# Attention with P times V in five rounds a head, issued in two places, and one partial sum moved to VectorE

## The reference

```python
# layer 0 (per batch, 16 heads of 32)
energy = jnp.einsum('bhqd,bhkd->bhqk', q, k)
att = jax.nn.softmax(energy, axis=-1) / D ** 0.5
out = jnp.einsum('bhqk,bhkd->bhqd', att, v)
...
# layer 1
attn = jax.nn.softmax(jnp.einsum('bhqd,bhkd->bhqk', q, k) * hd ** (-0.5), axis=-1)
o = jnp.einsum('bhqk,bhkd->bhqd', attn, v).transpose(0, 2, 1, 3).reshape(B, T, D)
x = x + bitlinear(o, w_proj, b_proj)
```

## Time and profile before

| | |
|---|---|
| median of three executions | 3016.07 us |
| the profiled execution | 3021.92 us |
| its span | 3020.1 us |
| TensorE busy | 2781.6 us, 92% |
| VectorE busy | 2246.9 us, 74% |
| GpSimd busy | 1987.6 us, 66% |
| ScalarE busy | 1839.4 us, 61% |

### The profile page before, as it was taken

The page is one execution under the profiler, slowest core; times in us unless marked ns, Lnnn a source line. Parts: engine busy times, 40 slices in busy tenths (PEclk is TensorE's granted clock), DMA queues, the critical chain, the costliest instruction groups (busy, mean ns, idle before and its releaser), DMA issues. The chain is left out here.

```text
span 3020.1 us, 70269 instructions
## 1 busy us (share of the span) xinstructions
PE 2781.6 (92%) x22313; PEld 1481.0 (49%) x22313; DVE 2246.9 (74%) x4482; ACT 1839.4 (61%) x3287; POOL 1987.6 (66%) x1677
## 2 busy tenths in 40 slices
PE   7899999999999989999569998998999899958998
PEld 6654466444755547454235444544444445524444
DVE  4777688776877778777667768776877787738997
ACT  3366655665556654666346676667666766657887
POOL 0288824886268841889438885887788688854441
PEclk9999999999999999999889999999999999979999
DMA  6122343223422324222133213322232222143000
GB/s 210 43 54 53 125 133 100 54 69 120 154 70 58 116 105 131 63 53 74 40 108 81 55 23 107 80 58 53 79 75 58 64 73 61 39 152 134 31 28 35
DMA packets 101853, 243.28 MB, mean 81 GB/s; under 512 B 18620, under 2 KB 24900, under 8 KB 100552
## 3 DMA queue, kind: packets, MB, share of 16 engines
q1 hardware_dynamic: 99784, 233.49, 27.1%
q0 software_dynamic: 1792, 6.33, 0.6%
HBM read 99.15 MB, written 38.88 MB: 46 GB/s over the span
## 5 line engine op out<-in xcount | busy, mean ns | idle before, releaser
L459 DVE TENSOR_REDUCE b_mxs<-ps 128x1 f32<-128x512 f32 x1024 | 636.2, 684 | 198.4 <-PE ps L340 197.3
L459 DVE TENSOR_REDUCE a_mxs<-ps 128x1 f32<-128x512 f32 x1024 | 635.4, 683 | 176.7 <-PE ps L340 175.5
L425 ACT ACTIVATE a_p<-ps 128x512 f32<-128x512 f32 x1024 | 530.4, 602 | 242.3 <-PE ps L354 237.1
L425 ACT ACTIVATE b_p<-ps 128x512 f32<-128x512 f32 x1024 | 533.5, 602 | 201.3 <-PE ps L354 196.2
L312 POOL TENSOR_TENSOR b_sum<-b_p 128x512 f32<-128x512 f32 x384 | 496.7, 1297 | 87.2 <-ACT b_p L425 86.8
L312 POOL TENSOR_TENSOR a_sum<-a_p 128x512 f32<-128x512 f32 x384 | 498.2, 1301 | 68.6 <-ACT a_p L425 68.3
L340 PE MATMUL ps<-b_k,b_q 96*128 96x512 f32 x1024 | 443.6, 438 | 33.7 <-DVE b_mxs L459 23.3
L340 PE MATMUL ps<-a_k,a_q 96*128 96x512 f32 x1024 | 417.9, 417 | 6.8 <-DVE a_mxs L459 3.7
L354 PE MATMUL ps<-b_q,b_k 98*128 98x512 f32 x1024 | 400.1, 425 | 11.0 <-ACT b_p L425 7.8
L354 PE MATMUL ps<-a_q,a_k 98*128 98x512 f32 x1024 | 396.2, 421 | 9.8 <-ACT a_p L425 9.8
L368 PE MATMUL ps<-a_p,a_vx 128*32 128x512 f32 x2048 | 372.1, 599 | 10.7 <-POOL a_sum L317 8.9
(11 more groups left out here) (267 smaller groups left out, 4157.3 us busy)
## 6 DMA issues: line engine op xcount, KB each, us to landing
a_q<-a_qh SPq DMA_DIRECT2D x128, 128.0 KB, 2.3
a_k<-a_kh SPq DMA_DIRECT2D x128, 128.0 KB, 2.3
b_q<-b_qh SPq DMA_DIRECT2D x128, 128.0 KB, 2.3
b_k<-b_kh SPq DMA_DIRECT2D x128, 128.0 KB, 2.4
a_p<-in_w_fc SPq DMA_DIRECT2D x12, 1024.0 KB, 8.5
a_kl<-in_x SPq DMA_DIRECT2D x4, 2048.0 KB, 8.4
a_q<-a_ql SPq DMA_DIRECT2D x64, 128.0 KB, 2.3
a_k<-a_kl SPq DMA_DIRECT2D x64, 128.0 KB, 2.3
```

The costliest lines, as they stand in the source:

```text
L425: act.activation(self.key_tile(u, kt), self.st[RING[CHUNKS * (k % NJ) + n]], ACT.Exp, scale=self.scale).then_inc(self.s_exp, 1)
L459: dve.reduce_max(self.mxs[:, c:c + 1], self.mx[RING[CHUNKS * j + c]], axis=AX.X).then_inc(self.s_mxr, 1)
```

## The change

It changes how the eight key tiles of a half are dealt to rounds and who adds what.

- A table `VALUES` says for each of five rounds what each column group does: a pair (half, key tile), or (half, SUM). Rounds 0 and 1 do six key tiles of half 0 with two sums, round 2 does the last two of half 0 and the first two of half 1, rounds 3 and 4 do the other six of half 1 with its two sums. All twenty places are filled: 16 key tiles and four sums.
- A sum now covers four key tiles. Three of the four sums are POOL's (`SUM_OF` 0, 1 and 3), of three additions each. The fourth, of key tiles 0 to 3 of half 1, is one VectorE instruction (`sum_four`), a `tensor_reduce` that reads four tiles which lie 512 elements (2048 bytes) apart, one element of each in turn, and writes 512 sums.
- On TensorE the rounds stand in two places: rounds 3 and 4 of the head before after step 2, rounds 0, 1 and 2 after step 6. The folds go ahead of them. The transposition of the maxima moves from step 3 to step 4.
- `fold` has two forms, since the sum stands in the last column group for half 0 and in the first for half 1.
- In layer 0, VectorE waits ahead of the first attention for a DMA (`s_gout[3]`).

```diff
+    VALUES = (((0, 0), (0, 1), (0, 2), (0, SUM)), ((0, 3), (0, 4), (0, 5), (0, SUM)), ((0, 6), (0, 7), (1, 0), (1, 1)),
+              ((1, SUM), (1, 2), (1, 3), (1, 4)), ((1, SUM), (1, 5), (1, 6), (1, 7)))
+    ROUNDS = len(VALUES)
+    SUM_OF = (0, 1, None, 2, 3)
+    LAST = (2, 4)
+    FREED = ((0, 0, 0, 1, 1, 1, 2, 2), (3, 3, 3, 3, 4, 4, 4, 4))
+    def sums(self, pool, N, r, i):
+
+        u, kt = self.VALUES[r][0][0], TT // 2 * (r in (1, 4))
+        tile = self.sum[:, self.SUM_OF[r], :]
+        pool.wait_ge(self.s_pv, self.ROUNDS * (N - 1) + r + 1 + self.PV_CREDIT)
+        for n in range(1, TT // 2):
+            pool.wait_ge(self.s_exp, CHUNKS * N + TT * u + kt + n + 1 + self.EXP_CREDIT)
+            if n > 1:
+                pool.wait_ge(self.s_part, 2 * (3 * N + i) + n - 1)
+            add = pool.tensor_tensor(tile, self.key_tile(u, kt) if n == 1 else tile, self.key_tile(u, kt + n), ALU.add)
+            add.then_inc(self.s_part if n < TT // 2 - 1 else self.s_sum, 1)
...
             if ok(k):
-                self.sums(pool, k, N, 0)
+                self.sums(pool, N, 0, 0)
+                self.sums(pool, N, 1, 1)
             if ok(k + 1):
                 self.value(pool, 4 * i + k + 1, N + 1, (k + 1) % 2)
             if ok(k):
-                self.sums(pool, k, N, 1)
+                self.sums(pool, N, 4, 2)
...
-                after_values = s in (0, 2, 5)
+                after_values = s in (3, 7)
...
-                if s == 1 and ok(k - 1):
+                if s == 2 and ok(k - 1):
                     self.out_transpose(pe, 2 * N - 2, 0)
-                    self.values_round(pe, k - 1, N - 1, 1, 1)
-                    self.values_round(pe, k - 1, N - 1, 1, 2)
-                if s == 3 and ok(k + 1):
+                    self.values_round(pe, k - 1, N - 1, 3)
+                    self.values_round(pe, k - 1, N - 1, 4)
+                if s == 4 and ok(k + 1):
                     pe.wait_ge(self.s_o, 2 * N + 1)
                     self.m_transpose(pe, N + 1, 0)
-                if s == 4 and ok(k - 1):
+                if s == 6 and ok(k - 1):
                     self.out_transpose(pe, 2 * N - 1, 1)
-                if s == 4 and ok(k):
+                if s == 6 and ok(k):
                     if ok(k + 1):
                         pe.wait_ge(self.s_mrow, N + 2)
-                    self.values_round(pe, k, N, 0, 0)
-                    self.values_round(pe, k, N, 0, 1)
-                if s == 7 and ok(k):
-                    self.values_round(pe, k, N, 0, 2)
-                    self.values_round(pe, k, N, 1, 0)
+                    for r in range(3):
+                        self.values_round(pe, k, N, r)
...
+    def sum_four(self, dve, N):
+        dve.wait_ge(self.s_exp, CHUNKS * N + TT + TT // 2 + self.EXP_CREDIT)
+        dve.wait_ge(self.s_pv, self.ROUNDS * (N - 1) + 3 + 1 + self.PV_CREDIT)
+        keys = self.p[:, :, :].rearrange("p a (h n) -> p (a h) n", h=2)[:, TT:TT + TT // 2, :]
+        dve.tensor_reduce(self.sum[:, self.SUM_OF[3], :], keys.rearrange("p t n -> p n t"), AX.X, ALU.add).then_inc(self.s_sum_dve, 1)
```

More of the change, by code:

```diff
@@ L209, in setup_pool @@
         fill(self.ones[:, :], 1.0)
[L211 to L216, removed]
+        fill(self.fold[:, :, :], 0.0)
+        for u, sums in enumerate((3 * HD, 0)):
+            for r in range(0, P, HD):
+                if r != sums:
+                    ch.mark(pool.affine_select(out=self.fold[:, u, 0:HD], in_=self.fold[:, u, 0:HD], compare_op=ALU.not_equal,
+                                               fill=1.0, base=-r, pattern=[[-1, HD]], channel_multiplier=1))
+                    ch.wait()
+            fill(self.fold[sums:sums + 1, u, HD:HD + 1], 1.0)
         assert ch.n == self.SET
@@ L239, in call @@
             ok = (lambda kk: 0 <= 4 * i + kk < H) if known else (lambda kk: True)
-            head(i, k, H * b + n, ok, 5 if known and n == H else STEPS)
+            head(i, k, H * b + n, ok, 7 if known and n == H else STEPS)
         if flat:
@@ L355, in scores, with values_round @@
                   self.q[j][0:98, u * HALF:(u + 1) * HALF], start=True, stop=True).then_inc(self.s_st, 1)
[L357 removed]
+    def values_round(self, pe, k, N, r):
         if r == 0:
[L360 to L371 removed]
+            pe.wait_ge(self.s_o, 2 * N + 1)
+            pe.wait_ge(self.s_vx, N + 1)
+        if r == self.LAST[0]:
+            pe.wait_ge(self.s_o, 2 * N + 2)
+        if r == 3:
+            pe.wait_ge(self.s_sum_dve, N + 1)
+        elif self.SUM_OF[r] is not None:
+            pe.wait_ge(self.s_sum, 3 * N + (0, 1, None, None, 2)[r] + 1)
+        for c, (u, kt) in enumerate(self.VALUES[r]):
+            rounds = [n for n in range(self.ROUNDS) if self.VALUES[n][c][0] == u]
+            tile, weights = ((self.sum[:, self.SUM_OF[r], :], self.ones[:, :]) if kt == self.SUM else
+                             (self.key_tile(u, kt), self.vx[k % 2][:, kt, :]))
+            mm = pe.matmul(self.ot[u][HD * c:HD * (c + 1), :], weights, tile, start=r == rounds[0], stop=r == rounds[-1])
+        mm.then_inc(self.s_pv, 1)
     def out_transpose(self, pe, U, u):
@@ L444, in head @@
                     upper()
[L445 to L446 removed]
+                if s == 3 and ok(k - 1):
+                    self.out_copy(act, N - 1, 1)
+                if s == 7 and ok(k):
+                    self.out_copy(act, N, 0)
                 if ok(k):
@@ L492, in head @@
                 a = 1 if s < 2 else 2
-                if ok(k + a):
-                    for c in range(2):
+                for c in range(2):
+                    if ok(k + a):
                         self.reduce_chunk(dve, N + a, (k + a) % NJ, (2 * s + c + CHUNKS - 4) % CHUNKS)
+                    if s == 6 and c == 0 and ok(k - 1):
+                        self.divide(dve, 2 * N - 1, 1, 4 * i + k - 1)
                 if s == 1 and ok(k + 1):
                     self.m_parts(dve, N + 1)
-                if s in (1, 4) and ok(k - 1):
-                    self.divide(dve, 2 * N - 2 + s // 4, s // 4, 4 * i + k - 1)
+                if s == 2 and ok(k - 1):
+                    self.divide(dve, 2 * N - 2, 0, 4 * i + k - 1)
+                if s == 6 and ok(k):
+                    self.sum_four(dve, N)
                 if spare and ok(k) and not ok(k + 2) and (s >= 2 or not ok(k + 1)):
```

59 lines of the change are left out of this document (16 added, 43 removed).

## The result

| | before | after |
|---|---|---|
| median of four executions | 3018.53 us (3015.41 to 3026.71) | 3206.72 us (3203.92 to 3212.26) |
| span of the profiled execution | 3020.1 us | 3202.1 us |
| mean granted TensorE clock | 0.973 | 0.931 |

The ratio is 1.0621 with a 95% interval of 1.0593 to 1.0649: 188 us slower. The forecast was 2956 us, and its range ended at 3120.

A forecast was written before the change was run, and what follows sets the result against it. TensorE was taken to bound, 14.5 of 14.77 us a head. After the change, a POOL-TensorE-ScalarE chain (13.9), VectorE (13.6) and TensorE (13.35) gave 14.15 a head, 61 us saved, 2956 us; range 2938 to 3120, likeliest 2938 to 2971.

The forecast's parts named there:

- the price of `sum_four`: VectorE's reduction over four tiles, priced from a row over side-by-side elements (2286 ns) at 2.2 us net of overlap.
- the 3.1 us at which the sign turns: Reduction time from about which VectorE needs 14.4 us, a head takes 14.7, and the change makes the kernel slower.
- the likeliest range: The forecast's own case for the kernel's time, 2938 to 2971 us, chance 0.38.
- Rival A: VectorE's strided reduction is slow, 3.75 us; a head takes 15.4 us, the kernel 3095 us; chance 0.37.
- The loop: Chain through POOL (10.55 us), then TensorE and ScalarE (3.36 us), closing at the scores of step 7: 13.9 us a head.
- Rival B: POOL's additions stay 1.44 us apart, making the chain through three engines 14.3 us; 2972 to 2984 us; chance 0.16.
- the 0.1 to 0.5 named: Sign expected on TensorE: the second of the three rounds waits for POOL 0.1 to 0.5 us a head.
- VectorE's terms: VectorE's work a head: max reductions 9.6, maximum parts 0.54, divides 1.3, together 11.4 us; with the reduction at 2.2, 13.6.
- Three requirements lie close together: Per head, the chain through three engines needs 13.9 us, VectorE 13.6, TensorE 13.35; a head was taken as 14.15.
- small waits: The 0.3 us by which a head before the change exceeded TensorE's summed work, 14.5 us of 14.77.
- Rival C: POOL and VectorE hinder each other in SBUF, adding 0.7 us to the chain; 3010 to 3022 us; chance 0.05 with other cancellations.
- The last head: End of a batch, where TensorE makes no max chunks: the last head gives back 1.1 us of the gain per batch.

The follow-up runs named there:

- run 1: The changed kernel with VectorE's reduction summing four neighbouring elements instead of one from each of four tiles; sums not the softmax's; 2967.15 us, ratio 0.9824.
- run 3: The changed kernel with two reductions of two tiles each, 4096 bytes apart, in place of the one over four tiles; 2973.53 us in one execution.
- runs 2: The changed kernel with the reduction reading two neighbours of each of the four tiles, 2048 elements in, 256 sums out; 2964.11 us in one execution.
- run 10: The changed kernel with the four tiles interleaved in pairs (step of 8 bytes), the reduction reading two neighbours at each place; computes the reference; 2980.58 us, ratio 0.9864.
- Run 9: The changed kernel with three of a head's max chunks, just ahead of TensorE's wait for VectorE, issued twice; 3127.05 us, ratio 1.0341.
- run 13: The kernel of run 10 with one addition fewer in POOL's first sum of a head; results not the reference's; 2942.88 us, ratio 0.9744.
- run 11: The changed kernel with the reduction taking 508 sums of elements 2032 bytes apart instead of 2048; 3179.89 us in one execution.
- run 7: The changed kernel with VectorE's reduction made only in the first head of a batch; most outputs not the reference's; 2976.65 us, ratio 0.9848.
- run 14: The kernel of run 10 with round 2 behind step 7 instead of step 6; computes the reference; 2943.11 us, ratio 0.9741.
- run 4: The changed kernel with three VectorE additions in place of the reduction; results are the reference's; 3008.33 us, ratio 0.9961.

## Why the prediction was wrong

**The step that failed** is the price of `sum_four`: "The nearest row is the same instruction over 2048 elements that lie side by side, 2286 ns; I take it, 2.2 us net of overlap, since type, memory and count agree." Those three agree, but the order in which the elements are read does not, and it decides: 3.83 us for 2.28 (run 1). That is beyond the 3.1 us at which the sign turns. Run 1 has the order of the read alone put right, and the kernel comes in at 2967 us, inside the likeliest range. The contiguous row was called the nearest although it differs in the one thing that the change does anew.

The Trainium skill's page Vector Engine (DVE) Microarchitecture Reference, section 5.2 Measured stream behaviour on trn2, stood on the right side with its 1.73 ns a column for a source that hops every element; measured here 1.87 an element, whole instruction included. Its remark that a stream alternating between two regions keeps the full rate agrees with run 3 within a tenth (1.22 ns an element for 1.11 over neighbours), and its rule on adjacent pairs with runs 2 and 10. The error was to carry the remark from two places to four. The Trainium skill's page SBUF — State Buffer, section Specifications (TRN2), says of cachelines that each access that crosses to a new 16-byte line pays; run 3, in which every access does, shows almost no such cost, so it isn't that rule in this plain form.

**Rival A** was right in its mechanism and in its size: a reduction of 3.75 us (3.83), a head of 15.4 (15.33 at the full clock). That 3.75 lies so near is luck: it is four times a row of another instruction, with two inputs. What the rival lacked, and what took the time out of a range that held it, is the clock: the second step that failed is that every term was priced at a clock of 1.00. It gave 3095 us, and the kernel took 3207; 60 us of the middle heads are Rival A, 93 go with TensorE at 1.2 GHz. Run 9 gives 80 us back by adding work. The remaining 31 us, in first and last intervals and rests, I did not divide. The profile before had shown a clock of 1.00 only beside a TensorE at 99.5% and more, and I carried that over to a kernel in which TensorE would wait for VectorE in each head (16.8 us between matmuls in the batch of the window). What length or number of waits brings the clock down, these runs don't settle.

**The loop.** Where the read is fast it came out as forecast. Timeline, POOL, run 1:

```profile
527.07 2.64 POOL L321 TENSOR_TENSOR a_sum<-a_sum,a_p 128x512 f32<-128x512 f32 x2 [1.98 <-ACT a_p L428]
...
533.63 1.28 POOL L321 TENSOR_TENSOR a_sum<-a_p 128x512 f32<-128x512 f32 x1
534.99 2.65 POOL L321 TENSOR_TENSOR a_sum<-a_sum,a_p 128x512 f32<-128x512 f32 x2
...
541.08 2.64 POOL L321 TENSOR_TENSOR a_sum<-a_sum,a_p 128x512 f32<-128x512 f32 x2 [1.87 <-ACT a_p L428]
```

From 527.07 POOL works through to 534.99 + 2.65 = 537.64, which is 10.57 us (forecast 10.55); from there to 541.08, when the exponential of step 7 is there, are 3.44 us (forecast 3.36). Together 14.01 us, and the head is 14.07. Additions stand 1.36 us apart (533.63 to 534.99), so Rival B is out. The second of the three rounds waited for POOL as foreseen. In the middle heads of run 10 its first matmul with ones as weights starts 0.69 us after the last one of the round ahead, against 0.43 in all middle heads of run 13: 0.26 us a head, of the 0.1 to 0.5 named. (The 5.9 us in seven heads of the wait row are the weight loads', and TensorE loses less.)

**VectorE and TensorE.** 11.4 + 3.83 = 15.2 us against 15.33 a head confirms VectorE's terms; in run 11 a reduction shorter by 0.06 us goes with a head shorter by 0.06. That VectorE is no bound with the fast read is shown by run 7. "Three requirements lie close together" holds as well, and closer than forecast: run 13 takes 1.36 us out of the loop, the 0.26 us of waiting for POOL go, and the head stops 0.20 us further, at 13.98. So the loop costs a head about 0.2 us over the next limit. The forecast had 13.6 for VectorE and 13.35 for TensorE, with its 0.3 of small waits 13.9 and 13.65; which of the two stops the head at 13.98 is not tested. **Rival C** found no support in the change: in layer 0, POOL's additions that overlap the reduction took 1.27 to 1.28 us and the others 1.29 to 1.30.

**The last head.** The forecast gave back 1.1 us a batch. Run 1 shows more. Its middle heads save 13 x 0.68 = 8.8 us and the last interval 0.7, but the first costs 0.9, the rest in layer 0 grows by 3.3 us, in layer 1 by 0.4, and between the layers by 4.5. So 8.6 x 8 = 69 us less 16 leaves 53, against 61 forecast. With a fast read the forecast's own range, 2938 to 2971, holds run 1's 2967 us; run 10's 2981, the version that computes the reference, lies 10 us above it. Moving round 2 behind step 7 (run 14) takes the layer-0 rest back to 137.7 us, its value before.

## What to carry to other kernels

Take the price of a read from a row with the same order of elements; where there is none, an equal count is no evidence, and the far bound deserves the chance. When another engine becomes the bound, look at what TensorE's clock does once TensorE waits: price the heads at both levels. And a chain across engines that closes within the time of a stage can be added up from a timeline: here the sum was right to 0.1 us. Moving a round out of it (run 14 against run 10) was worth 37 us, nearly as much as the rest of the change with a fast read, but only 0.10 us in a middle head; half of it came at the ends of batches. And read TensorE's waits from its matmuls: the weight loads' row showed 0.84 us a head for POOL where, in the same window, the matmuls started 0.17 us later than without a wait.

## What the runs showed of the hardware

- A VectorE reduction in fp32 from SBUF took 1.11 ns an element over neighbours, 1.22 over two places in turn, 1.24 over three, 1.87 over four (3828 ns for 2048), and a distance of 2032 bytes in place of 2048 changed little (1.85). Two neighbours at each place brought it back to 1.11.
- TensorE's moving operand at a step of 8 bytes cost nothing to speak of (at most 0.65 us, for 0.59), at 16 bytes it took a matmul from 0.59 to about 1.1 us; ScalarE's write at 16 bytes went from 0.60 to near 1.1 us, at 8 bytes nearly nothing (608 ns for 602 as the mean of sixteen).
- Three matmuls a head issued twice made the kernel 80 us faster: TensorE fell to 1.2 GHz in 4% of the middle heads, for 54% without them.
- With two inputs in SBUF, an addition of VectorE took 1.07 us beside one of POOL and 0.69 alone (run 4); a reduction with one input left POOL's additions at 1.28 us.
